# Softmax denominators: VectorE adds the first three probability tiles of a unit in two places, GpSimd adds five more, and the ones product takes that one sum

## The reference

```python
def _L0_attn_ref(embeddings, w_qkv):
    result = (embeddings @ w_qkv).reshape(b, s, 3, NUM_HEADS, HEAD)
    q, k, v = ...   # each (b, heads, s, head)
    scores = jnp.einsum('bnqd,bnkd->bnqk', q, k) / jnp.sqrt(jnp.float32(h))
    probs = jax.nn.softmax(scores, axis=-1)
    ctx = jnp.einsum('bnqk,bnkd->bnqd', probs, v)
    return jnp.transpose(ctx, (0, 2, 1, 3)).reshape(b, s, h)

def _L0_ffn_ref(x, w_gate, w_up, w_down):
    gate = fp4_linear(x, w_gate)
    y = fp4_linear(x, w_up)
    return fp4_linear(jax.nn.silu(gate) * y, w_down)

x = _layernorm(x + _L0_attn_ref(x, L0_attn_w_qkv))
x = _layernorm(x + _L0_ffn_ref(x, w_gate, w_up, w_down))
```

## Time and profile before

| what | value |
|---|---|
| median of three runs | 3920.85 us (3920.46 to 3924.07) |
| the profiled execution, its own time | 3922.93 us |
| its span (first to last instruction) | 3921.3 us |
| mean granted clock of TensorE | 0.988 of full speed |
| PE busy | 3744.5 us, 95% |
| DVE busy | 3024.0 us, 77% |
| POOL busy | 2232.0 us, 57% |
| ACT busy | 1709.7 us, 44% |
| one batch (attention and feed-forward) | 463.5 us, from POOL's first addition in one batch at 662.97 us to that in the next at 1126.42 us |

### The profile page before, as it was taken

One profiled execution on the slowest core, in us unless ns is written; L12 is line 12 of the kernel. 1 busy time (PEld: TensorE's weight loads), 2 busy tenths in 40 slices (PEclk: granted clock), 3 DMA queues, 4 the chain that ended last, 5 costly groups with the idle time before them and its releaser, 6 DMA issues. The chain is left out here.

```text
span 3921.3 us, 61535 instructions
## 1 busy us (share of the span) xinstructions
PE 3744.5 (95%) x22853; PEld 1727.3 (44%) x22853; DVE 3024.0 (77%) x5075; ACT 1709.7 (44%) x3085; POOL 2232.0 (57%) x1427
## 2 busy tenths in 40 slices
PE   3599999999999999999999999999999999999999
PEld 2244454344544355443544445434454334544354
DVE  9876787678876688667877678767887668866787
ACT  2166423663246532555226542366424553255522
POOL 1298624984268832787229862398425883278722
PEclk9699999999999999999999999999999999999999
DMA  5211101011011110111101110101101111010110
GB/s 169 81 36 34 55 21 37 17 43 48 25 31 32 35 47 20 43 27 35 47 20 39 31 57 20 39 17 42 49 22 33 30 37 46 20 42 25 31 52 22
DMA packets 106565, 152.53 MB, mean 39 GB/s; under 512 B 28176, under 2 KB 55568, under 8 KB 106128
## 3 DMA queue, kind: packets, MB, share of 16 engines
q1 hardware_dynamic: 106256, 148.49, 12.2%
HBM read 76.28 MB, written 19.66 MB: 24 GB/s over the span
## 5 line engine op out<-in xcount | busy, mean ns | idle before, releaser
L604 DVE TENSOR_REDUCE mx<-R 128x1 f32<-128x512 f32 x2080 | 1316.9, 683 | 536.1 <-PE R L698 533.1
L1265 ACT ACTIVATE arena<-SC 128x512 f32<-128x512 f32 x1360 | 755.6, 603 | 407.9 <-PE SC L1531 279.2
L1606 PE MATMUL SC<-wgu,split 128*128 128x512 f16 (+1 forms) x3456 | 714.5, 361 | 0.0
L1176 POOL TENSOR_TENSOR arena<-arena,sc_h 128x704 f32<-128x704 bf16 (+1 forms) x144 | 178.0, 1250 | 606.1 <-DVE arena L528 606.1
L1150 POOL TENSOR_TENSOR wd<-wd,arena 128x1024 f32<-128x1024 f32 x212 | 494.2, 2358 | 44.5 <-ACT arena L1265 44.5
L1606 PEld LDWEIGHTS SC<-wgu,split 128*128 128x128 f16 x3456 | 338.3, 98 | 331.4
L1265 ACT ACTIVATE wd<-SC 128x512 f32<-128x512 f32 x688 | 389.8, 603 | 211.8 <-PE SC L1531 149.1
L1307 ACT ACTIVATE arena<-SC,gain 128x512 f32<-128x512 f32 (+1 forms) x192 | 125.1, 651 | 810.2 <-PE R L1606 411.9
L678 PE MATMUL R<-xT,wqkv 128*128 128x512 bf16 x1632 | 421.5, 380 | 19.5 <-DVE xT L591 13.1
L698 PE MATMUL R<-ks_even,qs_even 96*128 96x512 bf16 x1056 | 395.0, 389 | 27.6 <-DVE mx L604 7.8
L698 PE MATMUL R<-arena 96*128 96x512 bf16 x1024 | 374.0, 382 | 13.2 <-DVE xT L591 8.2
(11 more groups left out here) (138 smaller groups left out, 5496.6 us busy)
## 6 DMA issues: line engine op xcount, KB each, us to landing
x<-n_L_attn_embeddings_dram SPq DMA_DIRECT2D x136, 256.0 KB, 2.8
wd<-wd_kept SPq DMA_DIRECT2D x32, 512.0 KB, 5.4
out_dram<-x SPq DMA_DIRECT2D x64, 256.0 KB, 2.0
ks_even<-split SPq DMA_DIRECT2D x204, 64.0 KB, 2.0
qs_even<-split SPq DMA_DIRECT2D x408, 32.0 KB, 1.8
arena<-split SPq DMA_DIRECT2D x192, 64.0 KB, 2.0
arena<-split SPq DMA_DIRECT2D x384, 32.0 KB, 1.8
wd<-wd_kept SPq DMA_DIRECT2D x16, 384.0 KB, 7.2
```

Source lines behind the costliest of these rows:

```text
L604: nc.vector.reduce_max(mx[:, j:j + 1], ring_of(ring, job)[:, :], AX_X).then_inc(max_done, 1)
L1176: nc.gpsimd.tensor_tensor(blocks_of(q_h[:, cols]), blocks_of(r_h[:, cols]), spread(sc_h[:, c], c.stop - c.start), ALU.mult).then_inc(qh_do ...
L1265: nc.scalar.activation(probs_of(s)[:, hd, :], SC[e % SLOTS][:, :], ACT.Exp, scale=SCALE).then_inc(exp_done, 1)
L1606: last = nc.tensor.matmul(GU[kk % 2][which][:, 0:w], xhT[i % 2][:, part_x * KH + k, :], wgu[:, part_w * KH + k, which * I + first:which * ...
```

## The change

The first two pairs of a unit's additions move from POOL to DVE: a new function `first_sums(u, t)` on DVE adds tiles 0 and 1 (t = 1) and tile 2 (t = 2). It is called in steps 2 and 4 (`FIRST_SUM_STEPS`), each time right behind the second maximum of the step (`FIRST_SUM_MAX`), and signals a new semaphore `first_sum`. POOL goes on from tile 3 to tile 7 (to tile 5 in a batch's last unit), so it has 5 pairs (3) where it had 6 (4). The `sum` job loses one source: it reads `acc` alone, and in the last unit `acc` and tiles 6 and 7. ACT's wait for a free probability buffer follows (`probs_free`), and the waits on the previous output's stores move from POOL's first addition to DVE's.

```diff
--- before.py
+++ after.py
@@ -85,7 +85,9 @@
 
 
 QUARTERS = 4
-POOL_SUMS = [TILES - 2] * (UNITS - 1) + [TILES // 2]
+POOL_SUMS = [TILES - 1] * (UNITS - 1) + [TILES // 2 + 1]
+FIRST_SUM_STEPS, FIRST_SUM_MAX = {2: 1, 4: 2}, 2
+FIRST_SUMS = len(FIRST_SUM_STEPS)
 MAX_STEPS = (5, 5, 5, 5, 5, 4, 3, 0)
 MAX_STEPS_LAST = (5, 5, 5, 5, 5, 4, 1, 2)
 MADE = (((1, (4, 5)), (1, 1, 1, 1, 1, 1, 1, 1)), ((2, (0, 1)), (1, 1, 1, 1, 1, 1, 1, 1)),
@@ -423,6 +425,7 @@
         scores_done = sem("scores_done")
         exp_done = sem("exp_done")
         pv_done = sem("pv_done")
+        first_sum = sem("first_sum")
         pool_sum = sem("pool_sum")
         ctxT_done = sem("ctxT_done")
         sumT_done = sem("sumT_done")
@@ -466,7 +469,7 @@
 
         def sums_done(u, t, i):
 
-            return 2 * (sum(pool_sums(v) for v in range(u)) + t - 1) + i + 1
+            return 2 * (sum(pool_sums(v) - FIRST_SUMS for v in range(u)) + t - FIRST_SUMS - 1) + i + 1
 
         norms = [("x", 0), ("x", 1)]
         for i in range(TILES):
@@ -1137,17 +1140,11 @@
                     def sum_probs(u, t, i):
                         s, hs = TILES * u + t, slice(2 * i, 2 * i + 2)
                         pool.wait_ge(exp_done, GROUP * s + 2 * i + 2)
-                        if t == 1:
-                            if u >= 2:
-                                pool.wait_ge(ring_full, ring.full(("sum", u - 2, 0)))
-                            if u >= UNITS and u % UNITS == 0:
-                                for par in range(2):
-                                    pool.wait_ge(stored[par], 16 * TILES // 2 * (u // UNITS))
-                            first = probs_of(s - 1)[:, hs, :]
+                        if t == FIRST_SUMS + 1:
+                            pool.wait_ge(first_sum, 2 * (FIRST_SUMS * u + FIRST_SUMS - 1) + i + 1)
                         else:
                             pool.wait_ge(pool_sum, sums_done(u, t - 1, i))
-                            first = acc[u % 2][i]
-                        nc.gpsimd.tensor_tensor(acc[u % 2][i], first, probs_of(s)[:, hs, :], ALU.add).then_inc(pool_sum, 1)
+                        nc.gpsimd.tensor_tensor(acc[u % 2][i], acc[u % 2][i], probs_of(s)[:, hs, :], ALU.add).then_inc(pool_sum, 1)
 
                     def inverse_deviation(name, i):
 
@@ -1179,8 +1176,8 @@
                     def units(b):
                         for u in range(UNITS * b, UNITS * (b + 1)):
                             first, ends = u == UNITS * b, u == UNITS * (b + 1) - 1
-                            for t in range(1, pool_sums(u) + 1):
-                                if ends and t == pool_sums(u):
+                            for t in range(FIRST_SUMS + 1, pool_sums(u) + 1):
+                                if ends and t == pool_sums(u) - 1:
                                     inverse_deviation("x", TILES * b)
                                 for i in range(2):
                                     sum_probs(u, t, i)
@@ -1234,8 +1231,10 @@
                         if i == 0:
                             act.wait_ge(pv_done, s + 1)
                         u, t = divmod(s, TILES)
-                        if t <= pool_sums(u):
-                            act.wait_ge(pool_sum, sums_done(u, max(t, 1), i))
+                        if t <= FIRST_SUMS:
+                            act.wait_ge(first_sum, 2 * (FIRST_SUMS * u + max(t, 1) - 1) + i + 1)
+                        elif t <= pool_sums(u):
+                            act.wait_ge(pool_sum, sums_done(u, t, i))
                         else:
                             act.wait_ge(ring_full, ring.full(("sum", u, 0)))
 
@@ -1371,6 +1370,24 @@
                             rec[:, :, :].unsqueeze(3).to_broadcast([P, UNIT_TILES, GROUP, HD]),
                             ALU.mult).then_inc(ctx_done, 1)
 
+                    def first_sums(u, t):
+
+                        s = TILES * u + t
+                        if t == 1 and u >= 2:
+                            dve.wait_ge(ring_full, ring.full(("sum", u - 2, 0)))
+                        if t == 1 and u >= UNITS and u % UNITS == 0:
+                            dve.wait_ge(qx_done, TILES * (u // UNITS))
+                            for par in range(2):
+                                dve.wait_ge(stored[par], 16 * TILES // 2 * (u // UNITS))
+                        for i in range(2):
+                            hs = slice(2 * i, 2 * i + 2)
+                            dve.wait_ge(exp_done, GROUP * s + 2 * i + 2)
+                            if t > 1:
+                                dve.wait_ge(first_sum, 2 * (FIRST_SUMS * u + t - 2) + i + 1)
+                            first = probs_of(s - 1)[:, hs, :] if t == 1 else acc[u % 2][i]
+                            nc.vector.tensor_tensor(acc[u % 2][i], first, probs_of(s)[:, hs, :],
+                                                    ALU.add).then_inc(first_sum, 1)
+
                     def moments(name, i, src, free):
 
                         k = norm_slot(name, i)
@@ -1393,11 +1410,15 @@
                             if (u, t) == (last, LN_MOMENTS):
                                 dve.wait_ge(added, last)
                                 first_moments(TILES * b)
+                            n_max = 0
                             for kind, a, j in jobs:
                                 if kind == "proj3":
                                     projected_low(a, j)
                                 elif kind == "max":
                                     maximum(a, j)
+                                    n_max += 1
+                                    if t in FIRST_SUM_STEPS and n_max == FIRST_SUM_MAX:
+                                        first_sums(u, FIRST_SUM_STEPS[t])
                                 elif kind == "neg":
                                     maxima_transposed(a)
                                 elif kind == "sumT":
```

## The result

Four runs of the changed kernel took 4258.02 to 4271.46 us, median **4264.75 us**; four of the kernel before took 3920.46 to 3925.13, median 3922.46. The ratio is **1.0871, with an interval of 1.0856 to 1.0887**: slower by 8.7%. Predicted were 4289 us and a range of 4130 to 4410. The profiled execution took 4271.46 us, 348.5 more than that of the kernel before.

The account below looks back on a forecast made before the run. PE, busy 95%, sets the time, but would wait on the DVE, POOL, PE chain. Per batch 7.0 + 24.8 + 8.0 waits, minus 6.0 product, plus 12 clock: 45.8 us; eight batches 366, so 4289 us, range 4130 to 4410.

Parts of the forecast that it names:

- The chain: Middle units: DVE's second pair, five POOL pairs and the context delay PE's ones product; waits of 24.8 us per batch.
- T4: The moment at which DVE ends the second maximum of step 4; 21.33 us before the next S in the third unit.
- S: Start of PE's ones product in step 2; forecast at T4 + 26.8 us in the middle units.
- POOL waits for a running DVE instruction: At POOL's first addition, beside DVE's second half in step 4: held 1.0 us, bounds 0 and 1.2.
- The product: PE's ones product in each `sum` job loses one tile, 0.86 us; 7 x 0.86 = 6.0 us less per batch.
- The first unit: T4 to S grows from 19.5 to 26.5 us, with no context and 1.0 us late: a wait of 7.0.
- The clock: PE's clock falls to half behind 7 of 8 waits per batch, 1.7 us each: 12 us, bounds 0 and near 24.
- The last unit: POOL's late context and additions hold DVE's moments and `quantise_x`; transposition near T4 + 24 to 25: 8 us per batch.
- This costs nothing more: Step 4: DVE's pair makes it 1.5 us late, but something else is later still, so no cost is added.
- DVE slips in between two POOL additions: Rival, step 2: DVE's pair delays POOL's last addition and S 1.1 us in seven units; 62 us, 4351 us, chance 0.12.
- The chain alone: Rival: POOL does not wait for DVE, the clock stays up, last unit costs 5 us; 190 us, 4113 us, chance 0.10.
- Rival B: The experiments' rival: 256 more additions on DVE, which feeds PE's ring, make the loss; POOL's waiting is a symptom.

Follow-up runs that it names:

- the one-operand experiment: Against the changed kernel, the second half of DVE's step 4 pair becomes a row maximum, as long, with one SBUF input: 4192.97 us.
- the filler: Against the changed kernel, PE makes 5 to 18 unused matmuls before the ones product in a batch's first seven units: 4182.19 us.
- the kernel with steps 2 and 3: Against the changed kernel, DVE's second pair is called in step 3 instead of step 4, nothing else changed: 4088.78 us.

## Why the prediction was right

**The chain** (T4 + 26.8 for S) was right to 0.15 us in the six middle units of the second batch, and its terms nearly so: the additions at 2.32, the context 1.25, and DVE's pair ends at T4 + 2.27. POOL's free start, which the prediction put at T4 + 2.3, is 0.2 us earlier by its own rows (2.11), and the 0.15 us from POOL's end to PE's start were left out; the two small errors cancel. The experiments confirm it as the cause: 0.84 us taken out of its start came back in every unit, one pair less removed the wait at the ones product altogether.

**POOL waits for a running DVE instruction.** The prediction took 1.0 us between bounds of 0 and 1.2, with no row for that direction. Measured are 0.80 to 0.85 over the 64 units, and 0.82 to 0.90 by what the one-operand experiment took out. The Trainium skill (SBUF — State Buffer, "Who interferes with whom") says that a DVE instruction with two inputs in SBUF contends with a GpSimd one that reads SBUF, and that the first issuer keeps the shared ports for its whole length; the traces agree in both directions (5.51 instead of 4.68 us for POOL's pair, 2.67 instead of 1.22 for DVE's addition), and the one-operand experiment, with L1367 and L601 beside it, shows that for the additions it is the second SBUF operand that does it. It says nothing of the small TENSOR_SCALARs of `quantise_x`, which have one tensor in SBUF and are held too (rows of L517 and L519 below).

**The product**, -6.0 per batch, came to -6.0: with the clock held up by the filler the distances S to T4 are those of the kernel before less 0.86 in each unit.

**The first unit** agrees in part by luck. Its +6.92 us holds 1.0 us of a lost turn of POOL's that had been given to a rival (below), while the prediction's +7.0 holds T4's lateness of 1.0, which the ledger has in another row (0.8). Like for like it is 5.9 against 6.0, as five batches of eight show (25.47 us from T4 to S).

**The clock** was a little over-sized: 12 us for seven waits, measured 9.9 in the second batch and 11 in the mean of all, because the falls reach S to T4 in five intervals or six, not in seven. In the second batch the clock stayed up behind the ones products of units 6 and 7, though the second of them (at 977.49) had waited 3.09 us, as long as that of unit 5 (at 900.96), behind which it fell. Behind unit 6 (a wait of 1.3 us) it fell in no batch, behind unit 7 (3.0 to 3.1 us) in six of eight.

**The last unit**, 8 us: the moments stand at T4 + 8.0 (predicted 8.2), the transposition at T4 + 23.8 (24 to 25), the gate product 7.6 us later than before. DVE's timeline there shows `quantise_x` held among four additions of POOL, as the prediction had it from the earlier trace rows:

```profile
994.87 0.69 DVE L1394 BATCH_NORM_STATS2 stats<-x 128x6 f32<-128x512 f32 x1 [3.37 <-POOL x L1138]
...
999.98 1.82 DVE L517 TENSOR_SCALAR inv<-inv 128x32 f32<-128x32 f32 x1
1001.83 2.27 DVE L519 TENSOR_SCALAR sc_x<-sc_x 128x32 f32<-128x32 f32 x1
1004.14 2.80 DVE L525 TENSOR_TENSOR split<-x,inv 128x512 f32<-128x512 f32 x1
```

**What the prediction had wrong or incomplete.** "This costs nothing more", of DVE's lateness in step 4, is true only under the longer chain. With one pair less on POOL it and the side path come out, at 8.2 us per batch in the middle units. The side path itself, POOL late, ACT's buffer late, PE's score late, stood in the code (`probs_free`) and not in the prediction. It costs nothing in the changed kernel, because PE waits longer for the sum anyway, but it bounds what any repair of the chain can give.

**The rivals.** "DVE slips in between two POOL additions" happened in six units of 64: in the first unit of three batches (T4 to S 26.44 us, 25.47 in the other five) and in the third unit of three others (27.68 instead of 26.71). Where it happens, POOL's last addition takes 3.33 us instead of 2.36. So it costs 6 us in all, not 62. "The chain alone" failed by the clock (80 us) and by the wait for DVE (54). Rival B, DVE's load, is not enough: on its own side it shows in the kernel with steps 2 and 3, but the changed kernel's wait is released by POOL.

## What to carry to other kernels

Before moving work off the busiest engine, follow the chain that the moved work hangs on through one whole period, and compare when the consumer arrives with when the producer can be done. Work with a late start on a slow engine costs by its *start* and not by its load: POOL did less here and became the bound. The same idea paid when only the piece that fits into an existing gap was moved, and only in the units where the chain had slack; the ends of a loop want a setting of their own.

## What the runs showed of the hardware

**Who gets in at the end of an addition changes from batch to batch, and the recorded starts don't tell it.** In the first unit of the second batch DVE's addition starts at 741.58 and POOL's last at 741.83, 0.25 later; POOL's takes 3.33 us, so DVE's ran first. In the third batch it is the other way, with 0.27 us between the two starts. POOL's timeline there:

```profile
1248.66 2.34 POOL L1147 TENSOR_TENSOR spill<-spill,wd 128x1024 f32<-128x1024 f32 x1
```

and DVE's:

```profile
1248.39 4.83 DVE L1388 TENSOR_TENSOR wd<-arena 128x1024 f32<-128x1024 f32 x2
```

The 0.02 us between the two cases are not the reason. In the first and third units of the eight batches DVE and POOL meet so 16 times, with DVE's start recorded 0.18 to 0.28 us ahead of POOL's. DVE runs first in 6 of them and POOL in 10, and a lead of 0.24 us stands with either outcome. In this kernel the order of the two is not safe to build on where both come to a boundary together.

**More work on PE made the kernel faster.** 608 filler matmuls of 0.38 us (576 of them are in the trace), and 83 us less time. In the second batch PE's waits of 2.2 to 4.4 us at the first five ones products went with 3.4 or 6.8 us at the lower of the two clock levels, right where the path hangs on PE; a wait of 1.3 us and one of 3.1 us did not. The same wait of 3.1 us did bring a fall in six other batches (S to T4 10.7 to 11.0 us there instead of 9.35), so the length of the wait alone does not tell it.
